# Four gated cross-attention layers on one core: attentions that begin by batch, and maxima spread four heads ahead

## The chip, the cores and the metric

The kernel runs on one core of a Trainium2 chip. The metric is the device time of one execution in microseconds (us). Engines are TensorE (PE, with its weight loads as PEld), VectorE (DVE), ScalarE (ACT), GpSimd (POOL) and SyncE (SP, which here issues DMAs). Each engine runs its own queue in order; they wait for each other by semaphores.

## The reference, cut to what matters

```python
x = x + tanh(g_xattn[0]) * xattn0(layernorm(x), ctx, mask)     # softmax over keys, mask of query x key
x = x + tanh(g_ffn[0])   * ffn0(layernorm(x))                  # 8 experts, each takes its top 256 tokens
x = x + tanh(g_xattn[1]) * xattn1(layernorm(x), ctx)           # softmax over the heads
x = x + tanh(g_ffn[1])   * ffn1(layernorm(x))                  # product of int8-quantised operands
x = x + tanh(g_xattn[2]) * xattn2(layernorm(x), ctx, padding)  # softmax over keys
x = x + tanh(g_ffn[2])   * ffn2(layernorm(x))                  # ternary weights, 256-1024-1024-1024-256
x = x + tanh(g_xattn[3]) * xattn3(layernorm(x), ctx)           # softmax over the queries
x = x + tanh(g_ffn[3])   * ffn3(layernorm(x))                  # 8 experts, two for each token
```

x and ctx are 8 x 256 x 256 (batch, rows, width) in fp32; every attention has 16 heads of width 16.

## The kernel before

All 2048 rows of x stay in SBUF as 16 tiles of 128 rows; a *pair* is the two tiles of one batch. The eight layers follow each other; each engine has a function for each (`attention`, `ffn0` to `ffn3`), run in the order of `STAGES`.

Layernorm: VectorE takes statistics of a tile (`statistics`, L1766, right behind each residual), then a chain of nine small operations for all 16 tiles at once with one square root on ScalarE (`layernorm`, L1782 to L1792), then normalises pair by pair (`normed`, L1816). TensorE transposes a pair (`turn_normed`, L751) and ScalarE copies it to `XNT` (L1434). Ahead of an attention, pairs 0 to 3 are done first and pairs 4 to 7 behind the first projections.

An attention projects keys, queries and values of a batch on TensorE (L804, L822, L842). ScalarE takes keys and queries out of PSUM (`split_k`, `split_q`), and ScalarE and VectorE split them into three bf16 parts (`middle_*`, `rest_*`, `low_*`; L1857, L1862, L1866, L1870). Six DMAs from POOL's queue (L337) and six from SP's (L474) then pack the parts of all heads into `Kpack` and `Qpack`, 128 KB each, so that one bf16 product of 96 rows gives exact scores. Rings of three batches.

Attentions 0 and 2 (`keys`): TensorE makes scores with the queries on the partitions (`smax`, L859), into two PSUM banks; VectorE takes row maxima (`row_max`, L1904). In attention 0 a second product with the identity adds the mask (L862). The maxima of a batch are turned (`max_turn`, L873), split into two bf16 rows (`max_part` on ScalarE, `max_rest` on VectorE, L1909) and written into `Qpack` by two DMAs (`max_rows`, L490), so that the second scores with the keys on the partitions (`scores`, L888, mask L891) come out less their maximum; ScalarE takes exponentials (`exps`, L1486), TensorE multiplies with the values (`values`, L897). `slot_keys(b)` on each engine writes out the order of a batch: the maxima of batch b + 1 (six of them ahead of the first score, then one behind each score), the scores of b, the end of b - 1, the projections of b + 3. `divide`, `output_turn`, `output_back`, `output` and `residual` (L1957) close a batch.

Attention 1 works in 16 units of 128 rows (`unit1`), attention 3 in eight slots (`slot3`, column maxima `col_max` L1914, four banks).

On SP, `attention` first waits for x of the layer before (`ready_x`), then issues the loads of context, weights and biases. `ffn1` issues the loads that copy 11 MB of feed-forward 2's weights from DRAM to DRAM (`staged`); `ffn2` loads them. `ffn0` gathers and scatters rows in DRAM and reads x back at its end (L418).

## Time and profile before

| | us |
|---|---|
| median of 3 runs | 2004.47 |
| lowest, highest | 1999.73, 2005.33 |
| profiled execution | 2003.19 |
| its span | 2001.3 |
| busy PE, DVE, ACT, POOL | 1635.1, 1091.8, 836.1, 295.8 |

The span runs from the first to the last instruction of the profiled execution. Times of the timeline count from its start. In it attention 0 runs to about 279, feed-forward 0 to 479, attention 1 to 774, feed-forward 1 to 826, attention 2 to 1081, feed-forward 2 to 1443, attention 3 to about 1640 and feed-forward 3 to the end. A matmul's duration in the rows holds its latency; where several follow each other, the distance of their starts is what one costs.

### The profile page before, as it was taken

The page shows a single profiled execution, that of the slowest core. Times are in us where ns is not written, and L with a number is a line of the kernel's source. Part 1 is how long each engine was busy: PE and PEld are TensorE (multiplying, and loading weights), DVE is VectorE, ACT ScalarE, POOL GpSimd, SP SyncE. Part 2 cuts the span into 40 slices and gives each one's busy share as a digit, 9 for nine tenths or more (in the row PEclk, how much of TensorE's full clock was granted, in tenths as well). Part 3 has the DMA queues.
Part 4 walks back from the last instruction along what each step waited for, and adds up shares of the span by engine and source line. Part 5 has one row for each costly group of instructions (what it writes and reads, how often), then busy time and mean ns, then how long its engine had stood idle before and what let it go on. Part 6 is the DMA issues. An engine that isn't in the chain of part 4 may idle for free.

```text
span 2001.3 us, 29422 instructions
## 1 busy us (share of the span) xinstructions
PE 1635.1 (82%) x10560; PEld 1228.3 (61%) x10561; DVE 1091.8 (55%) x2125; ACT 836.1 (42%) x1848; POOL 295.8 (15%) x351
## 2 busy tenths in 40 slices
PE   4999971794778874478887999999979873999997
PEld 3677750683555542335554677787745452999997
DVE  5555627404699998656663444535469966222221
ACT  3554440232776742335554622212289951222221
POOL 1100000432121100101110000000022201233332
PEclk8999985897798977679998999999989975999999
DMA  7545232125633315465523100000186625422221
GB/s 149 70 69 79 39 128 120 35 40 116 95 49 58 49 15 181 120 87 76 70 33 156 80 1 0 1 1 1 31 122 99 109 70 207 156 37 37 37 37 27
DMA packets 82841, 144.32 MB, mean 72 GB/s; under 512 B 13930, under 2 KB 68722, under 8 KB 79346
## 3 DMA queue, kind: packets, MB, share of 16 engines
q1 hardware_dynamic: 62754, 102.86, 22.1%
q0 software_dynamic: 19968, 39.87, 12.7%
q8 instruction: 76, 1.25, 0.3%
q14 instruction: 43, 0.35, 0.1%
HBM read 75.63 MB, written 27.79 MB: 52 GB/s over the span
## 4 chain that ended last, share of the span: by engine, by line
PE 60%; DVE 24%; ACT 5%; issue 5%; DMA 4%; SPq 1%; POOL 0%; DVEq 0%; POOLq 0%; ACTq 0%
PE ps L1259 12%; PE ps L1364 7%; PE ps L1375 7%; PE ps L897 4%; PE ps L1246 3%; PE ps L948 3%; DVE probs L2001 3%; DVE mx L1904 3%; PE ps L888 3%; PE ps L1179 2%; PE ps L1169 2%; PE ps L859 2%; ACT pT L1491 2%; PE ps L751 2%; PE ps L804 2%
## 5 line engine op out<-in xcount | busy, mean ns | idle before, releaser
L1904 DVE TENSOR_REDUCE mx<-ps 128x2 f32<-128x512 f32 x256 | 170.2, 688 | 149.2 <-PE ps L862 76.0
L337 POOL DMA_DIRECT2D Kpack<-KP x192 | 101.4, 536 | 984.8 <-DVE KP L1866 913.5
L1486 ACT ACTIVATE pT<-ps 128x512 f32<-128x512 f32 x256 | 146.0, 595 | 167.0 <-PE ps L891 91.4
L888 PE MATMUL ps<-Qpack,Kpack 99*128 99x256 bf16 (+1 forms) x768 | 163.8, 283 | 29.5 <-ACT pT L1491 11.4
L859 PE MATMUL ps<-Kpack,Qpack 97*128 97x256 bf16 x512 | 118.4, 292 | 49.1 <-DVE mx L1904 27.0
L1364 PEld LDWEIGHTS ps<-xgT,XNT 128*128 128x128 f32 x1280 | 150.3, 193 | 2.0
L1364 PE MATMUL ps<-xgT,XNT 128*128 128x128 f32 x1280 | 150.4, 276 | 0.0
L1375 PE MATMUL ps<-w,mid 128*128 x640 | 144.6, 379 | 0.0
L1693 ACT ACTIVATE mid<-ps 128x512 f32<-128x512 f32 x80 | 43.4, 595 | 206.9 <-PE ps L1364 206.9
L888 PEld LDWEIGHTS ps<-Qpack,Kpack 99*128 99x128 bf16 (+1 forms) x768 | 67.8, 100 | 99.3 <-ACT pT L1491 38.5
L1491 ACT ACTIVATE pT<-ps,nmax 128x256 f32<-128x256 f32 x256 | 120.2, 551 | 19.1 <-DVE nmax L1914 18.7
L1375 PEld LDWEIGHTS ps<-w,mid 128*128 128x128 f32 x640 | 118.6, 190 | 14.4
L1259 PE MATMUL ps<-partB,h 128*128 128x512 f32 x512 | 119.9, 395 | 1.3 <-ACT xn L1668 1.3
L1259 PE MATMUL ps<-partA,h 128*128 128x512 f32 x512 | 120.3, 396 | 0.0
L897 PE MATMUL ps<-pT,V 128*32 128x256 f32 x1536 | 112.0, 407 | 8.9 <-ACT pT L1486 6.5
L1259 PEld LDWEIGHTS ps<-partB,h 128*128 128x128 f32 x512 | 96.2, 188 | 24.3 <-ACT xn L1668 1.4
L1259 PEld LDWEIGHTS ps<-partA,h 128*128 128x128 f32 x512 | 96.3, 188 | 23.3 <-issue 0.5
L1668 ACT ACTIVATE xn<-ps,sc 128x512 f32<-128x512 f32 x64 | 43.2, 687 | 156.6 <-PE ps L1259 156.6
L1500 ACT ACTIVATE probs<-ps 128x512 f32<-128x512 f32 x128 | 77.3, 616 | 65.4 <-PE ps L980 65.0
L859 PEld LDWEIGHTS ps<-Kpack,Qpack 97*128 97x128 bf16 x512 | 45.9, 101 | 90.0 <-DVE mx L1904 61.7
L978 PE MATMUL ps<-Qpack,Kpack 96*128 96x256 bf16 x256 | 69.9, 296 | 30.9 <-DVE m L1976 28.7
L751 PE MATMUL ps<-ident,xn 128*128 128x128 f32 x224 | 41.9, 354 | 62.0 <-DVE xn L1816 52.7
(302 smaller groups left out, 3305.4 us busy)
## 6 DMA issues: line engine op xcount, KB each, us to landing
Kpack<-KP POOLq DMA_DIRECT2D x192, 128.0 KB, 5.2
Qpack<-QP SPq DMA_DIRECT2D x192, 128.0 KB, 7.1
w<-in_w SPq DMA_DIRECT2D x16, 1024.0 KB, 6.0
ctxT<-in_ctxT SPq DMA_DIRECT2D x32, 256.0 KB, 7.6
h<-h_rows SPq DMA_DIRECT2D x2, 4096.0 KB, 22.2
wd<-in_wd SPq DMA_DIRECT2D x4, 1536.0 KB, 14.4
xn_rows<-xn SPq DMA_DIRECT2D x16, 256.0 KB, 2.5
wu<-in_wu SPq DMA_DIRECT2D x4, 768.0 KB, 11.2
```

Source lines behind the costliest of these rows:

```text
L337: eng.dma_start(Kpack[j][DH * k:DH * (k + 1)].rearrange("d (e f) t -> d e (f t)", f=HALF), KP[par][:, part]).then_inc(done, 16)
L751: last = pe.transpose(bank[:, c, tt * P:(tt + 1) * P], src[:, tt, c * P:(c + 1) * P], eye[:])
L859: mm = pe.matmul(A[2 + h % 2][:, t], Qpack[j][0:MASK_ROW + 1, h, t * P:(t + 1) * P], Kpack[j][0:MASK_ROW + 1, h], start=True, stop=L != 0)
L888: mm = pe.matmul(A[h % ring][:, t], Kpack[par][0:rows, h, t * P:(t + 1) * P], Qpack[par][0:rows, h], start=True, stop=L != 0)
L897: mm = pe.matmul(O[c // 2][r0:r0 + VW, c % 2], V[par][:, t, h], weights[:, t], start=t == 0, stop=t == ST - 1)
L1259: mm = pe.matmul(bank, as_read(w[:, c, o * P:(o + 1) * P], x16), as_read(part[:, v, c], x16), start=v + c == 0, stop=v == 1 and c == HT - 1)
L1364: mm = pe.matmul(bank[:, f % 4 * P:(f % 4 + 1) * P], w1_tile[k % 2][:, c, f * P:(f + 1) * P], xgT3[k % 2][:, c], start=c == 0, stop=c == K ...
L1375: mm = pe.matmul(ps[5 + 2 * (k % 2)][:, 0], mid3[k % 2][:, c], w2_3[:, ds(e, 1), c].squeeze(1), start=c == 0, stop=c == HT - 1)
L1486: act.activation(pT[h % 8][:], A[h % 2][:], ACT.Exp).then_inc(s["exp_done"], 1)
L1491: e = act.activation(pT[h][:, t], A[h % 4][:, t], ACT.Exp, bias=nmax[:, t, h:h + 1], accum_out=esum[:, t, h:h + 1])
L1500: act.activation(probs[u % PROB_RING][:, 2 * k:2 * k + 2], A[(n_ - 1) % 4][:], ACT.Exp).then_inc(s["sc1_done"], 1)
L1904: dve.tensor_reduce(mx[:, :, h], A[2 + h % 2][:], AX.X, ALU.max).then_inc(s["smax_done"], 1)
```

## The change

- The layernorm of an attention begins with its first pairs (`HEAD`: one for attentions 0 and 1, two for 2 and 3). The chain is run twice, for the first tiles and for the rest (`deviations`), and pairs are normalised, transposed and copied one by one (`normed_pair`, `turn_pair`, `pair_out`); the rest of them stands behind the first scores: in attentions 0 and 2 inside `slot_keys`, in attention 1 inside `unit1` 0 and 1, in attention 3 inside `slot3(0)`.
- x is loaded in pieces of 2, 7 and 7 tiles, at the start and behind feed-forward 0.
- First keys (attention 1), or first keys and queries (attentions 2, 3), are projected and split inside the feed-forward ahead. For this the buffers of weights, context and splits (`pre`) no longer share memory with feed-forward 0 and 1, and SP issues the loads (`loads`) earlier: for attention 1 before it waits for feed-forward 0's scatters, for attention 2 at the start of feed-forward 1, for attention 3 in the last chunk of feed-forward 2.
- The DRAM to DRAM copies of feed-forward 2's weights go from the start of feed-forward 1 into attention 1's slots, three to five DMAs a batch.
- Attentions 0 and 2: the maxima run four heads ahead of the scores in one sequence over all batches (`MAX_AHEAD`), one maximum and one score in turn; the other steps of a slot get new places on all engines.
- Attention 0: the maxima's product with the mask (L862) goes; the mask is added on VectorE, in a `tensor_tensor_reduce` for each half of a head in place of one `tensor_reduce` for both.

```diff
@@ -42,6 +42,9 @@
 SOFTMAX_KEYS = (0, 2)
 PACK_RING, CTX_RING = 3, 4
 PROB_RING, UNITS1, AHEAD1 = 3, B * ST, 3
+HEAD = {0: 1, 1: 1, 2: 2, 3: 2}
+MAX_AHEAD = 4
+X_PIECES = (0, 2, 9, NT)
...
                         sp.wait_ge(s["v_psum"], 8 * i + b + 1)
                         load_ctx(b + CTX_RING, b % CTX_RING)
+                    for name in staged_in[b]:
+                        sp.dma_start(staged[name][:, b % HT], a[name][:, b % HT]).then_inc(s["f2_staged"], 16)

                 if L == 1:
                     packs1(0)
@@ -534,6 +567,8 @@
                         sp.wait_ge(s["xn_ready"], PAIRS * n + LNB * t + j + 1)
                         sp.dma_start(normed[:, ds(ST * (LNB * t + j), ST)], xn[j][:]).then_inc(xn_out[j], 16)

+            staged_in = [["h1_2", "h2_2", "w3_2"] + ["w1_2", "w2_2"] * (b < KC) for b in range(B)]
             def ffn(n, L):
...
@@ -737,6 +773,15 @@

             rt_order = {L: i for i, L in enumerate([L for k, L in stages if k == "ffn" and L in (0, 3)])}

+            def turn_pair(n, pair):
+                L = stages[n][1]
+                pe.wait_ge(s["xn_ready"], PAIRS * n + pair + 1)
+                pe.wait_ge(s["xnt_done"], PAIRS * n + LNB + max(pair - 1, 0))
+                for tt in range(ST):
+                    for c in range(KC):
+                        last = pe.transpose(turned_in(L, pair)[:, c, tt * P:(tt + 1) * P], normed_in(L, pair)[:, tt, c * P:(c + 1) * P], ident[:])
...
+                                       Kpack[j][0:MASK_ROW + 1, h], start=True, stop=True)
                     mm.then_inc(s["smax_ps"], 1)
+                def turn_later(b):
+                    pe.wait_ge(s["smax_done"], 16 * (8 * m_order[L] + b - 3) + H - 1)
+                    turn_pair(n, b)
...
-                pe.wait_ge(s["xnt_done"], PAIRS * n + LNB + 1)
-                proj_q(0)
-                for pair in range(LNB, PAIRS):
-                    turn_normed(n, LNB, pair - LNB)
-                pe.wait_ge(s["w_loaded"], w_total)
-                proj_v(0, 0)
-                proj_k(1, 1, 0)
-                pe.wait_ge(s["xnt_done"], PAIRS * (n + 1) + LNB)
-                proj_q(1)
                 if L == 0:
-                    pe.wait_ge(s["mask_ready"], 1)
+                    pe.wait_ge(s["qk_loaded"], qk_total(i))
+                    proj_k(0, 0, 0)
+                if HEAD[L] == 1:
+                    turn_pair(n, 0)
+                    proj_q(0)
+                    proj_k(1, 1, 0)
+                    turn_pair(n, 1)
+                    proj_q(1)
+                elif L == 3:
+                    pe.wait_ge(s["q_evac"], 8 * i + 2)
+                    pe.wait_ge(s["k_evac"], 8 * i + 2)
+                if not keys:
+                    pe.wait_ge(s["w_loaded"], w_total)
+                    proj_v(0, 0)
+                if L == 3:
+                    pe.wait_ge(s["f2_y"], NT)
                 if keys:
                     for h in range(H):
                         smax(0, h)
+                        if h == 3:
+                            pe.wait_ge(s["w_loaded"], w_total)
+                            proj_v(0, 0)
+                        if h == 7:
+                            turn_pair(n, 2)
+                        if h == 9:
+                            turn_pair(n, 3)
+                        if h == 11:
+                            proj_k(2, 2, 0)
                     max_turn(0)
-                    proj_k(2, 2, 0)
+                    for h in range(MAX_AHEAD):
+                        smax(1, h)
                     proj_q(2)
+                    if L == 0:
+                        pe.wait_ge(s["mask_ready"], 1)
...

                     def maximum(h):
-                        if nearer:
-                            smax(b + 1, h)
-                    maximum(0)
-                    maximum(1)
-                    if before:
-                        values(b - 1, 1 - par, CH - 1)
-                    for h in range(2, 6):
-                        maximum(h)
-                    if before:
-                        output_turn(b - 1)
-                    for h in range(10):
+                        if exists(b + 1 + h // H):
+                            smax(b + 1 + h // H, h % H)
+                    for h in range(H):
+                        maximum(h + MAX_AHEAD)
                         score(h)
-                        maximum(h + 6)
-                        if h == 3 and before:
-                            output_back(b - 1)
+                        if h == 1 and before:
+                            values(b - 1, 1 - par, CH - 1)
+                        if h == 4 and before:
+                            output_turn(b - 1)
                         if h == 5:
                             values(b, par, 0)
-                            if before:
-                                output(b - 1)
+                        if h == 6 and before:
+                            output_back(b - 1)
                         if h == 7 and nearer:
                             proj_v(b + 1, (b + 1) % CTX_RING)
-                    values(b, par, 1)
-                    score(10)
-                    if nearer:
-                        max_turn(b + 1)
-                    if later:
-                        proj_k(b + 3, (b + 3) % CTX_RING, (b + 3) // CTX_RING)
-                    score(11)
-                    score(12)
-                    if later:
-                        proj_q(b + 3)
-                    score(13)
-                    values(b, par, 2)
-                    score(14)
-                    score(15)
+                        if h == 8 and before:
+                            output(b - 1)
+                        if h == 9:
+                            values(b, par, 1)
+                        if h == 11 and exists(b + LNB):
+                            turn_later(b + LNB)
+                        if h == 11 and later:
+                            proj_k(b + 3, (b + 3) % CTX_RING, (b + 3) // CTX_RING)
+                        if h == 11 and nearer:
+                            max_turn(b + 1)
...
+                for p in range(2):
+                    turn_pair(n + 1, p)
+                pair(3, 1, False)
+                proj_q(0)
+                pair(4, 0, False)
+                proj_q(1)
+                for b in range(5, B):
+                    pair(b, b % 2, False)

...
+                if HEAD[L] == 1:
+                    deviations(chains[n], slice(0, ST))
+                    if L == 0:
+                        split_k(0, 0, 0)
+                    pair_out(n, 0)
+                    if L == 0:
+                        middle_k(0, 0)
+                    split_q(0, 0, 0)
+                    middle_q(0, 0)
+                    if L == 0:
+                        act.wait_ge(s["gates_loaded"], 32)
+                        act.activation(tg[:], gb[:], ACT.Tanh).then_inc(s["tg_ready"], 1)
+                    split_k(1, 1, 0)
+                    deviations(chains[n] + 1, slice(ST, NT))
+                    pair_out(n, 1)
...

                 def slot_keys(b):
                     before, nearer, later = exists(b - 1), exists(b + 1), exists(b + 2)
                     par = b % 2
-                    if later:
-                        split_k(b + 2, par, 0)
-                    if before:
-                        outputs_out(b - 1, 1)
-                    if later:
-                        split_q(b + 2, par, 0)
-                        middle_k(b + 2, par)
-                        middle_q(b + 2, par)
                     for h in range(H):
                         exps(b, h)
-                        if h == 4 and before:
+                        if h == 0 and later:
+                            split_q(b + 2, par, 0)
+                        if h == 1 and later:
+                            middle_k(b + 2, par)
+                        if h == 2 and before:
+                            outputs_out(b - 1, 1)
+                        if h == 3 and later:
...
                     m = 8 * m_order[L] + b
                     dve.wait_ge(s["smax_ps"], 16 * m + h + 1)
-                    dve.tensor_reduce(mx[:, :, h], A[2 + h % 2][:], AX.X, ALU.max).then_inc(s["smax_done"], 1)
+                    if L != 0:
+                        dve.tensor_reduce(mx[:, :, h], A[2 + h % 2][:], AX.X, ALU.max).then_inc(s["smax_done"], 1)
+                        return
+                    masked = Vb[0][:].bitcast(BF16).rearrange("p t (k s) -> p (t k) s", s=S)
+                    for t in range(ST):
+                        e = dve.tensor_tensor_reduce(masked[:, 2 * (h % 2) + t], A[2 + h % 2][:, t], mask_bf[:, 0, t], 1.0, NEG_EXP,
+                                                     ALU.add, ALU.max, mx[:, t, h:h + 1])
+                    e.then_inc(s["smax_done"], 1)

...
-                    low_q(b, b)
-                    if b == 0:
+                if HEAD[L] == 1:
+                    if L == 0:
                         constants()
-                        take_values(0, 0)
+                    dve.wait_ge(s["x_load0"], 16 * (1 + L))
+                    for t in range(ST):
+                        statistics(t)
+                    deviations(n, chains[n], slice(0, ST))
+                    normed_pair(n, 0)
+                    if L == 0:
+                        biases(0)
+                        rest_k(0, 0)
+                        low_k(0, 0)
+                    rest_q(0, 0)
+                    low_q(0, 0)
+                    dve.wait_ge(s["x_load1"], 32 * (1 + L))
+                    for t in range(ST, NT):
+                        statistics(t)
+                    if L == 1:
+                        dve.sem_inc(s["x_ffn"], 1)
+                    deviations(n, chains[n] + 1, slice(ST, NT))
+                    normed_pair(n, 1)
+                    rest_k(1, 1)
+                    normed_pair(n, 2)
+                    low_k(1, 1)
+                    normed_pair(n, 3)
+                    rest_q(1, 1)
+                if L != 0:
+                    constants()
+                if L == 0:
+                    masks()
+                    low_q(1, 1)
+                    dve.wait_ge(s["mask_ready"], 1)
+                elif L == 1:
+                    output_bias()
+                    low_q(1, 1)
...
+                            output_bias()
+                            take_values(0, 0)
                     max_rest(0)
+                    rest_k(2, 0)
+                    for h in range(MAX_AHEAD):
+                        row_max(1, h)

                 def slot_keys(b):
                     before, nearer, later = exists(b - 1), exists(b + 1), exists(b + 2)
                     par = b % 2
                     for h in range(H):
-                        if nearer:
-                            row_max(b + 1, h)
+                        ahead = h + MAX_AHEAD
+                        if exists(b + 1 + ahead // H):
+                            row_max(b + 1 + ahead // H, ahead % H)
+                        if h == 1 and later:
+                            rest_q(b + 2, par)
                         if h == 2 and later:
-                            rest_k(b + 2, par)
+                            low_k(b + 2, par)
                         if h == 4 and later:
-                            rest_q(b + 2, par)
-                        if h == 5 and later:
-                            low_k(b + 2, par)
-                        if h == 6 and before:
+                            low_q(b + 2, par)
+                        if h == 5 and before:
                             divide(b - 1)
-                        if h == 7 and later:
-                            low_q(b + 2, par)
-                        if h == 12 and before:
+                        if h == 7 and exists(b + LNB):
+                            normed_pair(n, b + LNB)
+                        if h == 8 and nearer:
+                            take_values(b + 1, 1 - par)
+                        if h == 10 and before:
                             residual(b - 1)
                         if h == 13 and nearer:
-                            take_values(b + 1, 1 - par)
-                    if nearer:
-                        max_rest(b + 1)
+                            max_rest(b + 1)
...
+                pair(0, 0)
+                pair(1, 1)
+                rest_k(0, 0)
+                deviations(n + 1, chains[n + 1], slice(0, 2 * ST))
+                normed_pair(n + 1, 0)
+                normed_pair(n + 1, 1)
+                low_k(0, 0)
+                pair(2, 0)
+                rest_k(1, 1)
+                pair(3, 1)
+                low_k(1, 1)
```

## Rows read from the trace of the kernel before

**Rows 1.** Busy time by stretch: stretch, length, PE, PEld, DVE, ACT, POOL (instructions), clock, DMA share, GB/s.
```profile
61.00:216.00 155.00, 147.74 (x1271) 112.69 (x1272) 87.43 (x160) 81.55 (x160) 18.83 (x36) 1.00 0.52 75
...
550.00:740.00 190.00, 156.43 (x1160) 99.83 (x1158) 186.19 (x207) 125.96 (x251) 23.34 (x36) 0.91 0.30 45
...
886.00:1023.00 137.00, 114.40 (x868) 73.64 (x867) 82.16 (x162) 73.25 (x149) 23.58 (x36) 0.94 0.51 69
...
1500.00:1600.00 100.00, 89.09 (x665) 51.44 (x665) 91.60 (x192) 93.78 (x375) 23.30 (x36) 0.97 0.65 105
```

**Rows 2.** Timeline, start: start, us, engine, line, operation, out<-in, count [idle before <-releaser].
```profile
6.92 2.71 DVE L1766 BATCH_NORM_STATS2 ln_st<-X 128x6 f32<-128x256 f32 x8 [6.77 <-DMA X<-in_x]
...
14.25 2.67 DVE L1816 TENSOR_SCALAR xn<-X,ln_tmp 128x256 f32<-128x256 f32 x8
...
16.21 0.60 ACT L1434 ACTIVATE XNT<-ps 128x512 f32<-128x512 f32 x1 [2.28 <-PE ps L751]
...
25.92 0.69 DVE L1870 TENSOR_TENSOR QP<-qr,QP 128x512 bf16<-128x512 f32 x1
...
41.87 0.69 DVE L1904 TENSOR_REDUCE mx<-ps 128x2 f32<-128x512 f32 x1 [6.70 <-PE ps L862]
```

**Rows 3.** Timeline, attention 0 in the steady state: two residuals, and products.
```profile
187.29 0.74 DVE L1957 SCALAR_TENSOR_TENSOR X<-ps,tg,X 128x512 f32<-128x512 f32 x1
...
210.40 0.27 PE L862 MATMUL ps<-mask_bf,ident_bf 128*128 128x256 bf16 x1
210.51 0.27 PE L859 MATMUL ps<-Kpack,Qpack 97*128 97x256 bf16 x1
...
216.27 0.74 DVE L1957 SCALAR_TENSOR_TENSOR X<-ps,tg,X 128x512 f32<-128x512 f32 x1
...
216.36 1.89 PE L842 MATMUL ps<-wv,ctxT 128*128 128x256 f32 x8
```

**Rows 4.** Timeline: two-operand operations on VectorE, and an accumulator read on ScalarE.
```profile
207.54 0.76 DVE L1947 TENSOR_TENSOR Oq<-ps,rden 128x256 f32<-128x256 f32 x2
...
1472.20 0.19 ACT L1491 ACTIVATION_READ_ACCUMULATOR pT<-ps,nmax 128x1 f32 x1
1472.30 0.47 ACT L1491 ACTIVATE pT<-ps,nmax 128x256 f32<-128x256 f32 x1
```

**Rows 5.** Timeline of two residuals of attention 2; waits of PE in 890 to 1023.
```profile
995.98 0.74 DVE L1957 SCALAR_TENSOR_TENSOR X<-ps,tg,X 128x512 f32<-128x512 f32 x1
...
1023.35 0.74 DVE L1957 SCALAR_TENSOR_TENSOR X<-ps,tg,X 128x512 f32<-128x512 f32 x1
...
PE ps L859 <- DVE mx L1904: 13.5, 20, 1.1
PE ps L873 <- DVE mx L1904: 5.1, 5, 1.7
```

**Rows 6.** One packing in attention 2: POOL's timeline; DMA rate in 904 to 925, 40 slices.
```profile
903.96 3.36 POOL L337 DMA_DIRECT2D Kpack<-KP x6 [14.55 <-DVE KP L1866]
...
GB/s 0 0 148 195 211 164 141 125 148 103 111 129 187 90 115 115 148 107 176 105 146 127 146 132 139 172 153 10 0 0 0 0 16 16 0 0 0 0 0 0
```

**Rows 7.** Timeline: x read back, and the first score of attention 1.
```profile
467.60 1.00 SPq L418 DMA_DIRECT2D X<-x_rows  x2
...
505.64 4.88 PE L966 MATMUL ps<-Qpack,Kpack 96*128 96x256 bf16 x22 [9.48 <-DMA Qpack<-QP]
```

**Rows 8.** Timeline: feed-forward 1's first and last step, and attention 2's first maximum.
```profile
805.55 0.88 DVE L2284 SCALAR_TENSOR_TENSOR y<-ps,lscale,rscale 128x256 f32<-128x256 f32 x2 [3.73 <-PE ps L1205]
...
825.55 0.75 DVE L1766 BATCH_NORM_STATS2 ln_st<-X  x2
...
855.75 11.06 DVE L1904 TENSOR_REDUCE mx<-ps 128x2 f32<-128x512 f32 x16 [8.32 <-PE ps L859]
```

**Rows 9.** Timeline: feed-forward 2's last products, and attention 3's first column maximum.
```profile
1434.12 7.75 PE L1282 MATMUL ps<-w,partA 128*128 128x256 f32 x64
...
1471.10 0.69 DVE L1914 TENSOR_REDUCE nmax<-ps 128x2 f32<-128x512 f32 x1 [6.30 <-PE ps L888]
```

545 lines of the change are left out of this document (355 added, 190 removed).

## The prediction

> **What bounds the kernel now.** I read the page first, then a table of busy times by stretch, then for each attention the start (timeline), one slot in the steady state (timeline, waits) and the DMA view of one packing. The kernel is one dependent sequence of eight layers, so a stage is worth what its own bound engine gives. The stretches [rows 1] show four kinds of attention: in attention 0 TensorE is busy 147.7 of 155 us; in attention 2 it is busy 114.4 of 137 at a clock of 0.94, no engine is full; in attention 1 VectorE is full (186.2 of 190); in attention 3 ScalarE and VectorE nearly are (93.8 and 91.6 of 100). Ahead of each attention lies a stretch of some 28 to 50 us in which nothing is full: the layernorm of all 16 tiles, first projections, splits, and the packing by DMA.
>
> **A. Start of attention 0.** Before, all 16 statistics (8 of them cost 2.71 us), all eight normalised pairs (a pair about 0.67) and both splits stand ahead of the first maximum, which begins at 41.87; the split of batch 0's queries had ended at 26.6 (25.92 + 0.69) [rows 2]. After, pair 0 goes alone: x in a piece of 256 KB lands at about 4, keys are projected and split before the queries; I put the query split of batch 0 at 18.6 (statistics 0.7, the chain to the deviation 1.5, pair 0.7, key product on the cold clock 2.6, transposes 1, copy 0.6, query product 2, four half-wide activations 1.6, three more steps of 0.65 each, and the key's steps queued between on ScalarE). Then VectorE must do 14 statistics (4.8), a second chain (1.5) and pair 1 (0.7) before batch 1 can be projected and split, which the order of VectorE puts ahead of the first maximum, with the mask conversions (0.8): 18.6 + 7 to pair 1, + 5.5 to its split queries, + 2.3: first maximum at about 33.4. That is 8.5 earlier. Packing is no longer last: keys of batch 0 travel during the layernorm, and the queries alone take half of what [rows 6] shows for both. The tanh and its table change lie under VectorE's statistics. Of the 8.5 I take 8; bounds 5 and 12.
>
> **B. Attention 0, mask in the maximum.** Removed on TensorE: the mask product of the maxima, 2 a head, 256 in all. Neighbouring matmuls start 0.11 apart [rows 3], so 32 x 0.11 = 3.6 us of a slot of 29.0 (two residuals apart [rows 3]). Added: two tensor_tensor_reduce of 128x256 a head in place of one tensor_reduce of 128x512, which costs 0.69 [rows 2]. The trace has no tensor_tensor_reduce. From below: two tensor_tensor of as many elements out of PSUM take 0.76 [rows 4]. From above I take twice that, 1.5, in case the reduction halves the rate. ScalarE reads its accumulator in a row of its own, 0.19 long, 0.10 to the next start [rows 4]; if VectorE does the same, a head costs 2 x (0.35 + 0.10) = 0.90, and I take that, as the structure is the nearest. VectorE's other work in a slot is four splits at 0.61, divide 1.15, residual with statistics 1.5, values 0.8, maximum row 0.4 and now a pair 0.67: 7.2. VectorE then has 16 x 0.90 + 7.2 = 21.6 a slot, TensorE 29.0 - 3.6 + 0.45 (a pair's transposes, moved here) = 25.9 with the 2 us of gaps it has now. The queues now alternate one maximum and one score, with ScalarE's query split, two middles and an output copy in the first four heads: exponentials 5 x 0.55 and this 3.9 against TensorE's 5.3, a stall of about 1. So 26.5 to 27 a slot: 2.2 x 5 full slots, 2.5 in slot 5 and 1 in slot 6, where VectorE (18.2) takes over from TensorE (16.1): 14. Bounds: -8 (1.46 a head, VectorE 30.6 a slot) and 24.
>
> The Trainium skill, "VectorE: DVE Perf Modes", section on the errata (fixed extra latency per instruction), speaks against this edit: every VectorE instruction out of PSUM pays 120 cycles plus one per element, so two halves cost more than one whole. By its figures two of 256 are an estimated 0.78 us against 0.66 for one of 512, 2 us more of VectorE in a slot. The rows agree on the direction (0.76 in [rows 4] to 0.69 in [rows 2]). The same page, on two instructions with no wait between them, counts an instruction that writes an accumulator as two; no row here shows that on VectorE.
>
> **C. Attention 2, maxima spread.** A slot lasts 27.4 and TensorE waits for maxima 13.5 + 5.1 us in 133 by the list of waits [rows 5], 3.8 a slot, and more through weight loads. Before, six maxima come in a bunch on two banks. Spread, TensorE's filler work lies between them. Its own work is about 20 at full clock. What is late next: ScalarE in the first four heads (6.6 against 4.2 on TensorE, 2.4), the row of maxima, which now leaves VectorE at head 13 and needs two DMA issues and 1.8 us to land, some 3.0, against 2.5 of product, maxima and score queued behind it (0.6). So I count 2.8 a slot for five slots and 2 in total behind: 16. Bounds 3 and 30.
>
> Maximum b+2 now begins at head 12 of slot b, so both packings must have landed by then. One packing takes 14 us from the key's first issue at 120 to 140 GB/s [rows 6]; key split at 3.5 in the slot, so 17.5, and TensorE reaches head 12 at 16 to 18. I cost it at 0; without that cover it is 1 to 4 a slot.
>
> **D. Attention 1.** The load is issued at 467.60 and the first product comes at 505.64 [rows 7]. After, the first 256 KB land about 2.8 us before the first megabyte did, weights and keys are ready, and the chain is: pair 0 split 10.5, 14 statistics and chain and pair 1 another 6.9, its transposes, copy, product, split 5.5, values 1.9: 24.8 behind 470.4, so 495.2, 10.4 earlier. Four pairs (2.7 us) move under a full VectorE [rows 1]: net 7.5; bounds 2 and 12. The copies of feed-forward 2's weights (11 MB) move from the transition into SP's queue behind each batch; SP's next packing waits some 20 us for its split there, so I cost them at 0.
>
> **E. From feed-forward 1 to attention 2.** First result 805.55, last statistics end at 826.3, first maximum 855.75 [rows 8]. After, keys, queries, splits and packing of batches 0 and 1 run inside feed-forward 1. The first result comes 1.9 later (a key product ahead), VectorE has 20.8 as before + 8 splits 5 + chain 1.5 + two pairs 1.35, + 1 of waits: it ends at about 837.4. The queries of batch 0 are split 9 us before that and land in time. With the two memsets (1.0) the first maximum is at 838.6: 17; bounds 12 and 20. Six pairs and a chain move behind the scores; the two among them that fall in the maxima of batch 0 are paid back by a product and a transposition less before the first score.
>
> **F. From feed-forward 2 to attention 3.** TensorE is full in feed-forward 2, so two pairs (1.0) and four projections (4 x 1.75, [rows 3] has 1.89 for eight) lengthen it by 8.1. The last layer's products began at 1434.12 [rows 9], so packing begins at 1442.2 and both packings take 13.5: first column maximum at 1456.4 against 1471.10, 14.7. Against it: ScalarE waits for the second chain ahead of its first exponential and loads its table then (3.0), and six copies of 0.60 fall in its full slot 0 (3.6): 8; bounds 3 and 15.
>
> **Sum.** 8 + 14 + 16 + 7.5 + 17 + 8 = 70.5. The profiled execution took 2003.19 (span 2001.3): 1932.7; the median of the runs is 1.3 above it, so 1934.
>
> **Rivals.** (1) VectorE bounds attention 0, at 1.3 to 1.5 us a head: B gives +3 to -8, so the gain is 48 to 60, time 1951, chance 0.13. For it: two instructions for one, no row. Against: two operations of that size at 0.76 [rows 4]. (2) Packing comes late for head 12 or the maxima row late for the first score: 2 to 3 a slot in both, C 4, B 5: 1955, chance 0.15. For it the 17.5 against 16 to 18. (3) Attentions 1 and 3 take back what their starts gave, as their engines are full: D 2, F 3: 1944, chance 0.10. (4) It does more than I count: all engines fill TensorE's gaps, B 24, C 30: 1910, chance 0.07. (5) Slower than before: a tensor_tensor_reduce of 128x256 that takes 0.9 us or more, 3 to 4 cycles an element. Attention 0 would be 128 heads x 1.8 + 7 x 7.2 + 17 for the last slot = 298 from the first maximum, against 237 now; that eats the 56.5 of the other parts. At 1.1 us it is 2060. Chance 0.07, of which 0.05 slower and 0.02 the same. (6) The forecast: 0.48.
>
> A measurement of this kernel can tell about 0.3% from no change. Faster 0.93, same 0.02, slower 0.05. The range takes in rivals 1 to 3 and 4 in part, and B and C at their low ends together: 1895 to 1970.
>
> **What would show it.** A: first maximum at 33, not 42. B: tensor_tensor_reduce near 0.4 with a short row behind it, slots of 26.5 to 27. C: slots of 24.6, waits of TensorE for maxima under 1 a slot. D, E, F: first score 25, first maximum 33 after feed-forward 1's first result, first column maximum 22 after the last layer's first product. Wrong if TensorE waits at head 12 for a DMA, if a slot of attention 0 has VectorE over 95% busy, or if attentions 1 and 3 are longer by more than 5 us from first score to end.

## The result and the profile after

The changed kernel took 1978.52 us (median of 4 runs, 1970.61 to 1979.44) where the kernel before took 2004.9 on the same chip: a ratio of 0.9864, interval 0.9832 to 0.9896. A second set gave 1982.12 (6 runs) against 2001.65: 0.9892, interval 0.9869 to 0.9916. So it is 20 to 26 us faster, not 70, and beyond the upper end of the range (1970).

The two profiled executions of the changed kernel (spans 1977.2 and 1980.8) against the one before, by the milestones that the forecast used; lengths in us:

```
stretch                                   forecast   before   after   after again
start to attention 0's first maximum        -8        41.9     35.0     36.6
attention 0, first maximum to last residual -14      236.5    235.3    238.0
last residual to feed-forward 0's logits     0        18.5     25.1     22.0
logits to attention 1's first score         -10.4    208.7    203.9    204.8
attention 1, first score to last residual   +2.7     267.5    271.2    268.2
to attention 2's first maximum              -17       82.7     65.8     65.7
attention 2, first maximum to last residual -16      224.1    219.8    219.6
to attention 3's first column maximum       -14.7    391.3    383.8    383.0
attention 3, first maximum to last residual +6.6     164.4    174.2    177.0
feed-forward 3                               0       365.8    363.1    366.0
```

One row is right to 0.1 us (E). Attention 0 gave 1.2 and -1.5 and attention 2 some 4.4, where 30 was counted for the two, attention 3 lost 10 to 13 us, and a stretch that the change doesn't touch, the routing of feed-forward 0, is 3.5 to 6.6 us longer. Apart from E's and most of A's, the gains are smaller than counted or given back elsewhere, so each had to be traced. Feed-forward 3, which no edit here touches, is between 360.0 and 366.1 long in the seventeen profiles of this document, so a difference of a few us in the total alone says little.

Busy times in the three attentions (columns as in [rows 1]). The kernel before:

```profile
41.87:278.40 236.53, 219.87 (x1860) 160.81 (x1858) 124.23 (x228) 114.89 (x222) 18.83 (x36) 0.99 0.42 62
855.75:1079.80 224.05, 183.01 (x1350) 112.26 (x1348) 127.51 (x248) 112.76 (x222) 29.26 (x44) 0.90 0.42 56
1471.10:1635.50 164.40, 143.79 (x1046) 83.29 (x1045) 137.97 (x293) 144.34 (x573) 29.02 (x44) 0.93 0.56 86
```

and the changed kernel:

```profile
34.97:270.30 235.33, 205.38 (x1636) 143.90 (x1636) 137.50 (x623) 115.16 (x228) 18.87 (x36) 0.94 0.39 60
836.30:1056.00 219.70, 180.15 (x1382) 116.79 (x1380) 133.97 (x274) 113.55 (x229) 29.34 (x44) 0.94 0.39 54
1439.87:1614.10 174.23, 145.61 (x1070) 86.12 (x1069) 143.91 (x315) 148.70 (x581) 29.08 (x44) 0.94 0.47 75
```

In attention 0 TensorE's busy time fell by 14.5 us, although 256 products at 0.11 (28 us) are gone: the granted clock fell from 0.99 to 0.94, and six pairs' transpositions (2.7) and a values product (1.9) now stand in this stretch. Its idle time rose from 16.7 to 30.0, which leaves 1.2 of the 14.5.

The slots themselves came out nearly as forecast. VectorE's timeline, residuals as in [rows 3] and [rows 5], and the new maximum:

```profile
35.32 0.42 DVE L2104 CUSTOM_DVE_ANT_0 Vb<-ps,mask_bf 128x256 bf16<-128x256 f32 x1
35.66 0.08 DVE L2104 DVE_READ_ACCUMULATOR2_ANT mx<- 128x1 f32 x1
35.66 0.42 DVE L2104 CUSTOM_DVE_ANT_0 Vb<-ps,mask_bf 128x256 bf16<-128x256 f32 x1
...
185.50 0.75 DVE L2159 SCALAR_TENSOR_TENSOR X<-ps,tg,X 128x512 f32<-128x512 f32 x1
...
212.02 0.75 DVE L2159 SCALAR_TENSOR_TENSOR X<-ps,tg,X 128x512 f32<-128x512 f32 x1
...
978.78 0.74 DVE L2159 SCALAR_TENSOR_TENSOR X<-ps,tg,X 128x512 f32<-128x512 f32 x1
...
1003.54 0.74 DVE L2159 SCALAR_TENSOR_TENSOR X<-ps,tg,X 128x512 f32<-128x512 f32 x1
```

Four full slots of attention 0 are 26.5, 28.3, 27.3 and 26.5 long where all were 29.0, those of attention 2 25.4, 24.8, 26.1 and 24.8 where they were 27.4. A tensor_tensor_reduce starts 0.35 after the one before it, the read of its accumulator (0.08) lies under the next one. What the slots gained, the stretch from the first maximum to the first residual gave back: 58.5 to 68.4 in attention 0 and 57.9 to 66.1 in attention 2. (The residual also stands three heads later in its slot, which moves a few us from the last distances into the first; the sums over an attention are free of that.)

### The profile page after: what moved, and what is told of

Read it like the earlier page. It is cut to its first block, busy times and chain, and to the rows that moved or that the text cites. A ratio compares the mean times of both kernels' runs of the same rounds, so it can differ in the third digit from the quotient of the medians.

```text
span 1977.2 us, 29280 instructions
## 1 busy us (share of the span) xinstructions
PE 1612.8 (82%) x10304; PEld 1214.1 (61%) x10305; DVE 1106.3 (56%) x2541; ACT 834.3 (42%) x1854; POOL 296.8 (15%) x351
## 4 chain that ended last, share of the span: by engine, by line
PE 56%; DVE 24%; ACT 7%; issue 6%; DMA 5%; SPq 1%; POOL 0%; DVEq 0%; POOLq 0%; ACTq 0%
PE ps L1361 12%; PE ps L1469 7%; PE ps L1480 7%; PE ps L1330 4%; DVE probs L2203 3%; DMA Qpack<-QP 3%; PE ps L1004 2%; PE ps L1241 2%; PE ps L861 2%; ACT pT L1605 2%; PE ps L1251 2%; PE ps L951 2%; PE ps L942 2%; PE ps L890 2%; PE ps L1386 2%
## 5 line engine op out<-in xcount | busy, mean ns | idle before, releaser
L1600 ACT ACTIVATE pT<-ps 128x512 f32<-128x512 f32 x256 | 151.9, 607 | 185.0 <-PE ps L945 98.0
L942 PE MATMUL ps<-Qpack,Kpack 99*128 99x256 bf16 (+1 forms) x768 | 166.4, 283 | 19.7 <-ACT pT L1605 9.9
L911 PE MATMUL ps<-Kpack,Qpack 97*128 97x256 bf16 x512 | 102.9, 287 | 40.4 <-DVE mx L2104 11.4
L1480 PEld LDWEIGHTS ps<-w,mid 128*128 128x128 f32 x640 | 118.6, 190 | 14.5
L2104 DVE CUSTOM_DVE_ANT_0 Vb<-ps,mask_bf 128x256 bf16<-128x256 f32 x256 | 94.8, 419 | 52.2 <-PE ps L911 52.1
L2100 DVE TENSOR_REDUCE mx<-ps 128x2 f32<-128x512 f32 x128 | 84.3, 686 | 46.2 <-PE ps L911 45.6
L2116 DVE TENSOR_REDUCE nmax<-ps 128x2 f32<-128x512 f32 x128 | 83.4, 683 | 26.2 <-PE ps L942 26.0
```

Source lines behind the costliest of these rows:

```text
L911: mm = pe.matmul(A[2 + h % 2][:, t], Qpack[j][0:MASK_ROW + 1, h, t * P:(t + 1) * P], Kpack[j][0:MASK_ROW + 1, h], start=True, stop=True)
L942: mm = pe.matmul(A[h % ring][:, t], Kpack[par][0:rows, h, t * P:(t + 1) * P], Qpack[par][0:rows, h], start=True, stop=L != 0)
L1480: mm = pe.matmul(ps[5 + 2 * (k % 2)][:, 0], mid3[k % 2][:, c], w2_3[:, ds(e, 1), c].squeeze(1), start=c == 0, stop=c == HT - 1)
L1600: act.activation(pT[h % 8][:], A[h % 2][:], ACT.Exp).then_inc(s["exp_done"], 1)
L2100: dve.tensor_reduce(mx[:, :, h], A[2 + h % 2][:], AX.X, ALU.max).then_inc(s["smax_done"], 1)
L2104: e = dve.tensor_tensor_reduce(masked[:, 2 * (h % 2) + t], A[2 + h % 2][:, t], mask_bf[:, 0, t], 1.0, NEG_EXP, ALU.add, ALU.max, mx[:, t, ...
```

## The experiments

All but e2 start from the changed kernel. For clock effects I use one figure, worked out from the tables of busy time by stretch: TensorE's busy time times (1 - granted clock), summed over pieces of half a microsecond. It is an estimate of how much of the busy time is there only because the clock was at 1.2 GHz (neighbouring products of 128x256 start 0.11 apart in [rows 3] and 0.21 apart in e5 from 82 to 84, where the granted clock is 0.50), and is called the low-clock part below.

In the total, e1 (0.9935) lies above the two sets of the changed kernel (ratios 0.9864 and 0.9892), e8 (0.9919) above the first and within the interval of the second, and e13, e14 and e15 lie below both. All other edits to it have 0.9871 to 0.9903, which can't be told from no change. What is said of those rests on stretches of one profile each.

### e1 and e2: the mask in the maximum (B), alone

```diff
-                                       Kpack[j][0:MASK_ROW + 1, h], start=True, stop=True)
+                                       Kpack[j][0:MASK_ROW + 1, h], start=True, stop=L != 0)
+                        if L == 0:
+                            mm = pe.matmul(A[2 + h % 2][:, t], ident_bf[:], mask_bf[:, 0, t], start=False, stop=True)
```

e1 has the products back (with tensor_reduce for every L). 

> The changed kernel with part B alone undone: in attention 0 the maxima get their mask products back (256 of them) and the tensor_reduce. Theory 1 (my forecast's step: the mask in the maximum is worth 14 us and lies on the path): 1978.5 + 14 = 1992, with full slots of 28.5 to 29 in attention 0. Theory 2 (the products removed were what kept TensorE dense, and the granted clock fell for it: in the changed kernel TensorE's records at the lower clock hold 9.6 us more extra time in attention 0 and 6.0 us more in feed-forward 0 than before): the 28 us of products come back, but some 12 to 15 of slow clock go, so attention 0 is within 4 us of the changed kernel's 235.3, feed-forward 0's way to the logits falls from 25.1 to about 18.5, and the total is 1972 to 1982.

e2 is the kernel before with this edit alone. 

> The kernel before with part B alone done: mask added inside the maximum in attention 0, nothing else. Forecast's theory: with maxima still in bunches, TensorE loses 3.6 us of work a slot, VectorE is not the bound (0.69 a head), so 2 to 3 a slot: 2004.5 - 20 = 1985. Clock theory: TensorE gets gaps, the granted clock of attention 0 falls from 0.99 to about 0.94 and feed-forward 0 loses up to 6.5: 1992 to 2000. In both the tensor_tensor_reduce costs 0.35 from start to start.

e1: 1986.54 (ratio 0.9935, 0.9914 to 0.9957). e2: 1997.41 (0.9980, 0.9965 to 0.9995). Attention 0 of e1 and of e2:

```profile
35.40:276.70 241.30, 220.73 (x1891) 165.94 (x1889) 129.62 (x239) 115.62 (x228) 18.83 (x36) 0.99 0.39 58
```

```profile
41.90:272.70 230.80, 201.61 (x1606) 137.39 (x1604) 132.14 (x611) 114.19 (x222) 18.84 (x36) 0.94 0.43 63
```

The edit is worth 5.7 us in attention 0 on the old order (236.5 to 230.8) and 5.2 on the new one (241.3 to 236.1, 236.1 being the mean of the nine profiles with this code of attention 0, from 234.3 to 238.2). Of 28 us of products, in e2 12.5 became idle time (16.7 to 29.2) and 9.4 low-clock part (2.1 to 11.5). In e1 the low-clock part is 1.6, in the nine profiles 8.7 to 15.0, and the three longest of these attentions have the three largest. So the clock theory was right about the clock, in both directions (0.99 with the products, 0.94 without), but too strong on the time: attention 0 does not stay as it was. By the ratios e1 is 9 to 14 us slower than the changed kernel. Only the 5.2 lie in attention 0; in its one profile the rest lies in stretches that the edit doesn't touch (attention 3 is 179.4 long, against 174.2 and 177.0), so the 9 to 14 is not the price of the edit.

### e3: the maxima of batch 2 behind slot 0

```diff
-                        maximum(h + MAX_AHEAD)
+                        if b or h + MAX_AHEAD < H:
+                            maximum(h + MAX_AHEAD)
...
+                    if b == 0:
+                        for h in range(MAX_AHEAD):
+                            maximum(H + h)
```

VectorE's maxima move in the same way.

> The changed kernel, only the four maxima of batch 2 that stand among the last scores of slot 0 (attentions 0 and 2) moved behind slot 0. If the DMA wait of 3.65 us at head 12 of attention 0's slot 0 (and its like in attention 2) is a loss of its own, the last four scores go out before it and about 3 us are gained there, 1 in attention 2: 1974.5. If it only moves (the same four maxima must still run before slot 1's), 0 to 1: 1978.

1973.95 (ratio 0.9897, 0.9862 to 0.9932), which by the ratio is no gain. The wait at head 12 of the changed kernel, by its list of waits in 58 to 100,

```profile
PE ps L911 <- DMA Qpack<-QP: 3.6, 1, 3.6
```

is gone, and the first exponential to the first residual of attention 0 takes 41.7 where the changed kernel has 44.0 and 45.3 (and no other profile with this slot 0 less than 43.6). Attention 2 shows nothing (221.0 to 219.7). So this wait costs 2 to 4 us, once, by one profile.

### e4 and e10: fillers on TensorE around feed-forward 0's routing

e4 puts 16 of 128x256 ahead of the first pair, e10 six of 128x128 behind each pair's router products:

```diff
+                if L == 0:
+                    for k in range(WARM0):
+                        pe.matmul(O[0][:, k % 2], ident_bf[:], mask_bf[:, 1, k % 2], start=True, stop=True)
...
+                if stages[n] == ("ffn", 0):
+                    for k in range(FILL0):
+                        pe.matmul(O[0][:, k % 2, 0:P], ident_bf[:], ident_bf[:], start=True, stop=True)
```

> The changed kernel with 16 matmuls of 128x256 that nobody reads put on TensorE's queue between attention 0's last output product and feed-forward 0's first transposition, where TensorE idles 4.9 us. Clock theory: feed-forward 0's transpositions and router products (25.1 us from the last residual to the logits, at a granted clock of 0.50 from 276 to 294; 18.6 in the kernel before, at up to 1.00) run at the full clock in part and save 3 to 6 us: 1973 to 1975. Rival (the fillers only delay, or the clock stays): 1978 to 1980.

> The changed kernel with 6 matmuls of 128x128 (bf16, nobody reads them) behind each pair's router products in feed-forward 0, where TensorE is busy without a gap for 20 us and yet runs at a granted clock of 0.50, the router products being only 8 columns wide. Theory a (what is granted follows the kind of work, and narrow products do not raise it): with wider work mixed in, the clock rises behind the first pairs and the stretch from the last residual to the logits takes 18 to 19.5 us in spite of 3 us more of work; total 1974 to 1978. Theory b (chance of the phase alone: 18.5, 22 or 25 in any kernel): the stretch is one of those, plus 3 to 5 us for the fillers: total 1981 to 1985.

The changed kernel in that stretch, and e10 (columns as in [rows 1]):

```profile
276.00:278.00 2.00, 2.00 (x12) 2.00 (x10) 1.26 (x5) 1.20 (x2) 0.00 (x0) 0.50 0.88 295
...
282.00:284.00 2.00, 2.00 (x11) 2.00 (x10) 0.00 (x0) 0.60 (x1) 0.00 (x0) 0.50 1.08 307
...
288.00:290.00 2.00, 2.00 (x11) 2.00 (x11) 0.00 (x0) 0.57 (x1) 0.00 (x0) 0.50 1.01 430
```

```profile
281.00:283.00 2.00, 2.00 (x13) 2.00 (x11) 1.26 (x4) 1.28 (x3) 0.00 (x0) 0.53 0.99 331
283.00:285.00 2.00, 2.00 (x24) 2.00 (x24) 1.91 (x7) 0.91 (x2) 0.00 (x0) 1.00 0.78 282
...
293.00:295.00 2.00, 1.36 (x17) 1.18 (x14) 0.71 (x3) 0.00 (x0) 0.00 (x0) 1.00 0.95 399
```

TensorE is busy without a gap in the changed kernel from 276 to 294 and stays at 1.2 GHz. The stretch took 18.5, 18.9, 21.7, 22.0 (nine times) or 25.1 us (three times) in the fifteen profiles without router fillers, with a low-clock part of 3.5, 6.7 or 10.0. With them it took 19.1 in e10 and 19.2 in e14 below, although TensorE has 48 products more to do, with a low-clock part of 1.4 and 1.5, less than any other. e4 had 22.0 like most: its fillers end before the pairs begin. So the fillers keep the clock up, on two profiles, as theory a had it. But the kind of work doesn't decide it alone: in the kernel before, the same instructions without fillers ran at 1.00 from 288 to 292. What decides between 18.5, 22.0 and 25.1 stays open. In the total neither edit shows: 1976.54 (0.9877) and 1977.83 (0.9895).

### e6 and e7: attention 3's packing, one batch after the other, or held

```diff
+                    if L == 2 and b == 1:
+                        sp.wait_ge(s["smax_ps"], 16 * 8 * m_order[L] + 1)
+                    if L == 3 and b == 1:
+                        sp.wait_ge(s["st_ps"], 16 * 8 * s_order[L] + 1)
                     queries_out(b, j)
```

This is e7 on SP's queue; GpSimd waits likewise ahead of pack_batch(1). e6 waits for batch 0's packing semaphores instead. e5, the changed kernel once more, ran beside them.

> The changed kernel as it is, for its median and for which of its losses come back in a second profile. Clock theory: the stretch from the last residual of attention 0 to the logits takes 18.5, 22.0 or 25.1 us from run to run of whatever kernel, in steps of about 3.3; total 1970 to 1980. The losses that belong to the program come back to 0.5 us: TensorE idle for 11 to 12 us before attention 3's values product and 5 us behind its first scores, and 3.6 us at head 12 of attention 0's slot 0.

> The changed kernel, with batch 1's packing begun in attentions 2 and 3 only when batch 0's has landed, so that the two no longer share the DMA engines. Theory 1 (attention 3's first score waits for packing): batch 0's twelve transfers land in about 8 us instead of 18 and the first column maximum comes 6 to 8 us earlier: 1971. Theory 2 (TensorE is held by its own instruction stream: it idles 11.6 us before the values product with no semaphore left to wait for, and goes on 1.8 us after one packet of 16 KB of the instruction queue, which travels while all 16 DMA engines are at 0.99): the engines are as full as before until both batches are packed, so nothing changes in attention 3: 0 to 2 us, 1976 to 1978. Attention 2 in both: first maximum bound by VectorE's last statistics at 834.7, so 1.5 earlier.

> The changed kernel, with batch 1's packing held until the first scores (attention 3) or the first maximum product (attention 2) of batch 0 have been issued. Theory 2 (instruction packets queued behind packing): the DMA engines run empty some 8 us after attention 3's packing begins, the packet comes at once, TensorE's idle time before the values product falls from 11.6 to 3 us or less and the 5.0 us behind the first scores may stay or move; first column maximum 8 us earlier, total 1969. Theory 1 (batch 0's packing alone): the same 8 us, so it is told from theory 2 by the run with serial packing beside it. Rival 3 (batch 1 now comes late for slot 1, or the later packs meet batch 2's): slot 0 of attention 3 is longer by as much: 1977.

Medians: e5 1982.12, e6 1972.73 (0.9871, 0.9847 to 0.9895), e7 1973.83 (0.9873, 0.9845 to 0.9901); the ratios are not clear of the changed kernel's. The chain of waits of the changed kernel there (start, length, what):

```profile
1417.94 6.12 PE ps L1386 x51
1424.07 11.58 issue
1435.65 3.75 PE ps L890 x8
1439.40 0.43 PE ps L942 x2
1439.83 0.43 PE ps L843
1440.26 4.99 issue
1445.25 0.59 PE ps L843
```

TensorE stands for 11.6 us ahead of the values product, whose semaphores had long been reached, and for 5.0 in the middle of one key product, between its two passes. e5 repeats both (10.6 and 4.7).

In the first of these stretches lies one instruction, a branch. Feed-forward 2's end stands in the program twice, in an `If` and its `Else` (L1401; L1297 in the kernel before, L1409 in e7), and TensorE leaves the one that ran by a jump over the other. The view of that line (duration of the four branches in ns, smallest, median and largest) in the kernel before, in the changed kernel and in e7:

```profile
L1297 PEldq COMPARE_BRANCH  x4: 79/1714/3416, 1118.1 to 1439.6; - x4
```

```profile
L1401 PEldq COMPARE_BRANCH  x4: 79/1954/13610, 1094.4 to 1421.8; - x4
```

```profile
L1409 PEldq COMPARE_BRANCH  x4: 79/1874/10530, 1088.7 to 1416.0; - x4
```

The largest is the last one in all three. It takes 3.4 us in the kernel before, where the DMA engines are at 0.02 and packing begins 17 us later, and 13.6 in the changed kernel, where packing began 5 us before it. In the half microsecond from 1432.0 the DMA view of the changed kernel has one packet of an instruction queue among the packing:

```profile
q8 instruction: 1, 0.02, 19.8%
```

It travels at 1432.2 and TensorE goes on at 1435.65; the next one is at 1442.8, before 1445.25. In all fifteen profiles of the changed order TensorE goes on 1.7 to 2.2 us after the first packet has ended, and in the ten with the second stall 1.2 to 1.7 us after the second one. In e7 the DMA engines run empty at 1424.0, and in the half microsecond up to there is TensorE's packet:

```profile
q8 instruction: 1, 0.02, 14.1%
```

```profile
1422.00:1424.00 2.00, 0.00 (x0) 0.00 (x0) 0.00 (x0) 0.00 (x0) 0.00 (x0) 0.50 1.13 168
1424.00:1426.00 2.00, 0.00 (x0) 0.00 (x0) 0.00 (x0) 0.00 (x0) 0.00 (x0) 0.50 0.02 6
```

```profile
1426.79 3.75 PE L898 MATMUL ps<-wv,ctxT 128*128 128x256 f32 x8 [8.50 <-issue]
1430.34 0.63 PE L950 MATMUL ps<-Qpack,Kpack 96*128 96x256 bf16 x2
1430.76 1.06 PE L851 MATMUL ps<-ctxT,wk 128*128 128x256 f32 x2
```

The second stall is gone there, the next packet (1427.2) finding idle engines; e6, which starts batch 1's packing as soon as batch 0's has landed, keeps it (4.1). So theory 2 holds in its second half: TensorE's instructions queue behind the packing. Its first half was too hopeful: the idle time fell only to 8.5 and the branch to 10.5, because batch 0's twelve transfers alone take until 1424.0. No run held batch 0's packing until the branch was past. Attention 3's first stretch (first column maximum to first residual) is 47.4 in e7 where e5 has 51.8 and e6 51.1, and its first maximum is 2.2 earlier. e4 and e10 confirm it: they differ from the changed kernel only by TensorE instructions in feed-forward 0, which shift where its packets end (this is also why I take the queue for TensorE's), and their stretches are 47.3 and 47.1, with no stall in the key product; all ten others in which batch 1's packing is not held (51.1 to 54.0) have it, 4.1 to 6.0 long. Attention 2 nets nothing in e6 and e7 (first maximum 1.6 earlier, then 1.4 more to the first exponential).

### e8: the weight copies back in feed-forward 1

```diff
-                    for name in staged_in[b]:
-                        sp.dma_start(staged[name][:, b % HT], a[name][:, b % HT]).then_inc(s["f2_staged"], 16)
...
                     sp.dma_start(rhs1[:], a["rhs1"]).then_inc(s["f1_rhs"], 16)
+                    for name in ternary:
+                        sp.dma_start(staged[name], a[name]).then_inc(s["f2_staged"], 16)
...
```

> The changed kernel with one thing undone: the copies of feed-forward 2's weights (11 MB) are issued in feed-forward 1 again and not behind each batch of attention 1. If they cost attention 1 what it gave back (first score to end 271.2 us against 267.5 before), attention 1 is 3 to 4 us shorter. In feed-forward 1 they now stand ahead of the packing of attention 2's first batches, so its first maximum comes 5 to 20 us later: total 1980 to 1995. If the copies are free in attention 1, its 271 stays, and only the second part is seen.

1985.48 (0.9919, 0.9899 to 0.9940). Attention 1 is 268.3, against 268.2 in e5, and attention 2's first maximum comes 10.4 later after attention 1's end (76.1 to 65.7). The copies are free where the change put them; my cost of 0 for them stands, and attention 1's give-back has another cause.

### e9 and e13: the way of the maximum row

```diff
-                        if h == 14 and later:
+                        if h == 15 and later:
                             proj_q(b + 3)
...
+                        if h == 12 and nearer:
+                            max_part(b + 1)
                         if h == 12 and exists(b + 3):
                             split_k(b + 3, 1 - par, 0)
-                        if h == 13 and nearer:
-                            max_part(b + 1)
```

The first edit alone is e9. The second, on ScalarE's queue, with VectorE's max_rest moved to h == 12 likewise, is e13.

> The changed kernel; in attentions 0 and 2 the query product of batch b+3 stands one head later, behind the last score of the slot and not behind score 14. In the changed kernel TensorE waits there for VectorE's rest of the maximum row, which frees the bank: 3.3 us in attention 0 and 5.1 in attention 2, waits that the kernel before did not have. If they are part of what ate the gain of the spread maxima, TensorE's idle time in attention 2's slots falls from 25 to 21 and the slots of 24.8 to 26.2 become 24 to 25: total 3 to 5 us less than the changed kernel. Rival: TensorE then waits as long for something else at that place (exponentials, the maximum row for the next slot's first score), and the slots stay within 0.2 us.

> The changed kernel; in attentions 0 and 2 ScalarE's and VectorE's two halves of the maximum row stand behind head 12 of the slot, ahead of the key split, not behind head 13, so that the row and the bank that it frees come one head and four activations earlier, some 2 to 3 us. If the way of the maximum row is what gives the spread's gain back (TensorE waits 5.1 us for that bank in attention 2 and 3.3 in attention 0, and when the query product was moved behind it, 5.0 and 3.3 for the row's DMA instead), both waits go: slots of 24.8 in attention 2 become 23.8, those of 27.3 in attention 0 become 26.5, and the kernel gains 6 to 10 us: 1970 to 1974 where the changed kernel has 1980. Rival: TensorE is then full or waits for exponentials in the same places: under 2 us.

TensorE's waits in attention 2 (what waited for what, us, times, longest) in the changed kernel, 905 to 1056:

```profile
PE ps L861 <- DVE MR L2111: 5.1, 4, 1.3
PE ps L927 <- DVE mx L2100: 4.3, 2, 2.2
...
PE ps L911 <- DVE mx L2100: 2.1, 4, 0.5
...
PE ps L942 <- DMA Qpack<-MR: 1.3, 1, 1.3
```

in e9, same stretch:

```profile
PE ps L942 <- DMA Qpack<-MR: 5.0, 6, 2.5
...
PE ps L861 <- DVE MR L2111: 0.8, 3, 0.3
```

and in e13, 897 to 1043, where the first of these lines is missing:

```profile
PE ps L942 <- DMA Qpack<-MR: 1.7, 2, 1.0
```

The spread took the 18.6 us of waits for maxima of [rows 5] down to 6.4, and a new one came: the query product waits for the bank that VectorE's rest of the maximum row frees. Moving the product (e9, 1979.64, 0.9903) turned it into a wait for the row's DMA, and attention 2's slots stayed (25.4, 24.8, 26.1, 25.6); attention 0's fell by 0.2. Moving the row itself one head and four activations forward (e13) cut slots to 23.8, 23.3, 24.6, 24.0 and 25.4, 25.4, 26.1, 25.4, and the total to 1966.71: 0.9818, 0.9792 to 0.9845. Attention 0 went from 236.1 (mean of nine) to 229.7, attention 2 from 219.6 to 216.0 (219.5 to 228.0 in the eight profiles with the changed kernel's attention 2). This one edit is worth 9 to 15 us by the ratios. It was rival (2)'s second half, which I had put at 0.6 a slot and 0.15 of chance.

### e11: x ahead of the keys' packing in attention 1

```diff
+                if L == 1:
+                    pool.wait_ge(s["x_load0"], 32)
                 pack_batch(0)
```

> The changed kernel; GpSimd packs the keys of attention 1's batch 0 only when the first piece of x has landed (now it issues them 1.3 us before x is loaded, and the first statistics begin 4.1 to 5.5 us after the load's issue, where my forecast had 2.8 for a quarter of the size). If the packing delays x, the first statistics begin 2.8 us after the issue and attention 1's first score 1.3 to 2.7 us earlier. Rival: no change, since the fixed part of a load is most of it, or the keys are packed too late, as the first maxima's product needs them 30 us later (they have room), 0.

1974.93 (0.9880, 0.9857 to 0.9904). In the changed kernel the load is issued at 465.82 and the statistics begin at 471.30; in e11:

```profile
462.54 1.50 SPq L442 DMA_DIRECT2D X<-x_rows  x3
...
465.68 3.29 POOL L345 DMA_DIRECT2D Kpack<-KP  x6 [5.23 <-DMA X<-x_rows]
...
465.41 0.75 DVE L1949 BATCH_NORM_STATS2 ln_st<-X 128x6 f32<-128x256 f32 x2 [4.21 <-DMA X<-x_rows]
```

2.9 us after the issue and not 4.1 to 5.5: the packing had delayed x. The first score comes 3.0 earlier (30.9 behind the load's issue, 33.9 in e5), and attention 1 is 271.1 long and not 268.2. That looks as if all of it were taken back, but the profile of the changed kernel and e4's have 271.2 too, without an earlier start, and slots of the same lengths: 1.0 more than e5 to the first residual and 2.0 more in the last four distances. Nor is the 3.0 firm: e14 below has this edit and its first score is 32.9 behind the issue, e13 doesn't have it and has 32.1. Together, from the routing's logits to attention 1's last residual, e11 takes 472.6, the changed kernel 475.1 and 473.0, the kernel before 476.2 and (e2) 473.7. So the edit gains nothing that can be told from no change.

### e12: attention 3's second chain first

```diff
-                        if b == 0 and h == 1:
-                            deviations(n, chains[n] + 1, slice(2 * ST, NT))
...
+                    deviations(n, chains[n] + 1, slice(2 * ST, NT))
                     slots_keys(slot3)
```

> The changed kernel; in attention 3 VectorE does the second chain of the layernorm's deviations ahead of the first column maximum, in its idle time of 10 to 13 us there, not behind the second maximum. In the changed kernel ScalarE waits for that chain and then loads its table ahead of its first exponential, which comes 9.2 to 9.5 us after the first column maximum against 0.7 in the kernel before. My forecast priced this at 3.0. If it is what makes slot 0 longer (first column maximum to first residual 51.9 against 39.2), the first exponential comes 1 us behind the first maximum and 5 to 8 us are gained: 1971 to 1974. If TensorE's own stall of 4.7 us behind the first scores (instruction packets) covers it, 1 to 3 us.

1978.7 (0.9897, 0.9878 to 0.9916). The first exponential, 9.5 us behind the first column maximum in the changed kernel (1449.38 to 1439.87), is 0.7 behind it (maximum at 1432.90):

```profile
1433.63 0.47 ACT L1605 ACTIVATE pT<-ps,nmax 128x256 f32<-128x256 f32 x1 [9.61 <-DVE nmax L2116]
```

and the first residual is not a microsecond earlier (52.1, e5 51.8): TensorE's stall in the key product is 6.0 here, and by that the one hides the other.

### e14 and e15: mended together

e15 is held packing, early row and chain first; e14 has x first and the router fillers as well.

> The changed kernel with the held second packing, attention 3's second chain ahead of its first maximum, x before the keys' packing in attention 1, the early maximum row and the router fillers together. By the single runs: held packing -7, early row -6 to -10 if it works, fillers 0 to -3, chain 0 alone but up to -5 where TensorE no longer stalls behind the first scores, x first 0: 1962 to 1968 where the changed kernel has 1980. If the attentions' engines take the starts back as in the run with x first, 1972.

> As the run before, without the router fillers and without x first. If the fillers are worth their 3 us in the long run (they keep the granted clock up in feed-forward 0) this one is 3 us slower than the run with them; if not, they are the same to 1 us. Also the second look at the chain put first in attention 3: with held packing its first exponential comes 1 us behind the first maximum and slot 0 is 3 to 5 us shorter than the 47.4 that held packing alone gave.

e14: 1955.0 (0.9758, 0.9731 to 0.9786). e15: 1953.76 (0.9752, 0.9732 to 0.9772), 49 us under the kernel before and about twice the gain of the change as it was. The three attentions in e15:

```profile
34.90:264.70 229.80, 204.20 (x1636) 144.37 (x1636) 137.63 (x623) 114.86 (x228) 18.85 (x36) 0.94 0.40 61
827.60:1042.10 214.50, 183.05 (x1380) 119.45 (x1380) 134.11 (x276) 113.61 (x229) 32.26 (x50) 0.92 0.44 59
1423.60:1589.60 166.00, 142.89 (x1070) 84.42 (x1068) 142.72 (x306) 146.99 (x579) 32.24 (x50) 0.96 0.56 87
```

Attention 3's first stretch is 44.0, 3.4 less than with held packing alone: with the stall gone the chain does cost, about the 3.0 that I had forecast. Fillers and x first together are worth nothing in the total, though e14's routing was 5.9 shorter than e15's in the profiles.

## Why the prediction was wrong, step by step

The two largest terms, B and C, failed by the same step: an attention was summed from its shorter slots, with its first stretch taken as unchanged and the late row of maxima at 0.6 a slot. They gave -1.5 to 1.2 and 4.4 where 30 was counted. F failed by the packing's length and by what else has to pass beside it, D by its load and its chain.

**A (8).** Right in kind: first maximum at 34.97 and 36.6, forecast 33.4, so 6.9 and 5.3. What it left out is that a values product (1.9) and six pairs (2.7 by the forecast's own 0.45 a pair) only moved behind the first maximum.

**B (14).** The slot of 26.5 to 27 came true (26.5 to 28.3), and 0.90 a head was too much: it is 0.69. The step that failed is the sum over an attention from its slots: 2.2 x 5 + 3 took the first stretch as unchanged. It is 9.9 to 11.9 longer, of which the later place of the residual is an estimated 5 (three heads of a slot of 26.5). There the moved work (1.9 + 2.7), the wait of 3.65 at head 12 (which I had costed at 0, for a cover of 17.5 against 16 to 18) and a part of the lower clock lie. Attention 0 as a whole gave 1.2 and -1.5. e2 shows the reason most plainly: removing work from the engine that bounds a stage opened gaps in it (12.5 of 28), and the granted clock fell with it (9.4 more). That it was the gaps which took the clock down is my reading; what e1 and e2 show is that it goes with the products.

**The routing behind it (0).** Not in my sum at all: 3.5 to 6.6 us. By the row-by-row clock it is the low-clock part (3.5 before, 6.7 and 10.0 after), and kernels with other edits show all three values. The kernel before was caught at the lowest; e2, which has the same code there, has 21.7. Executions of the changed kernel differ by 9 us in one set (1970.61 to 1979.44) and by 12 in the other (1973.29 to 1985.07), and the fastest had the highest mean clock (0.909 against 0.901 to 0.904 in the first set).

**C (16).** 4.3 and 4.5. "The row of maxima, which now leaves VectorE at head 13 ... (0.6)" is the term that was mis-sized: with the query product standing behind the same bank it held TensorE 5.1 + 1.3 us, and e13 got 3.6 of attention 2 and 6.4 of attention 0 back by it. As in B, the sum from the slots failed too: four full slots gave 8.6 together, 2.1 each where 2.8 was forecast, and the first stretch took 8.2 back. A part of that is the residual's later place, which the last slots return; another is moved work: at full clock TensorE has 5 us more to do in the stretch (180.15 less a low-clock part of 11.1, against 183.01 less 18.9). Of the 12 us that are missing, e13's 3.6 and this 5 make 9; the other 3 stay open. What remains of waits for maxima, 6.4, was forecast as under 1 a slot, rightly.

**D (7.5).** Two terms failed. The quarter load was not 2.8 faster: its statistics began 5.5 and 4.1 behind the issue where the whole megabyte had 5.6, because keys were being packed (e11 has 2.9). And the chain behind it, forecast at 24.8, took 28.0 and 29.9; TensorE's granted clock there was 0.63 and 0.62. Of the 3.9 to 4.8 that were left of 10.4, attention 1 took 0.7 to 3.7 back by the table. e8 rules the copies out. Attention 1's steady slots are 31.6 in every profile, before and after; what it gives back lies ahead of the first residual (95.5 before, 99.4 and 98.4 after), where the moved pairs are, forecast at 2.7. The length before is itself uncertain: e2, with the same attention 1, has 263.3 and not 267.4. By the sums over both stretches in e11's section D was worth -1.4 to 3.2, and the runs don't fix it closer.

**E (17).** 16.9 and 17.0. VectorE's last statistics of feed-forward 1 end at 833.6, two memsets at 834.7, first maximum at 836.30. That the sum is right to 0.1 is partly luck: the first result comes 3.3 later where 1.9 was forecast, VectorE takes 27.3 from there to its last statistics and not 30, and the first maximum is 2.7 behind them and not 1.2.

**F (8).** -2.3 and -4.3. "Both packings take 13.5" failed: that was the distance from batch 0's first issue to its first use (1456.87 to 1470.46). In the changed kernel batch 0's rows land 17.4 behind the first issue (1416.41 to 1433.83) and batch 1's 27.0; alone, in e7, batch 0's take 13.6. And the step took it that nothing but the packed rows is waited for. TensorE's branch out of feed-forward 2, done in 3.4 before packing began in the kernel before, now stands behind the packing and takes 13.6, the values product (3.75) comes behind it, and the stall of 5.0 in the first scores follows; none of this was in the sum. The 3.0 for ScalarE's chain was right in size, but only counts once that stall is gone (e12, e15).

**The rivals.** No single one came true. (2) did in both halves: the wait at head 12, once, and the late row in every slot. (3) did for attention 3 in size, but not by its reason: four slots are 19.7 to 20.0 long, 19.7 before, and the loss lies in the first stretch (39.2 to 51.9). Two mechanisms were not among the rivals, the clock and the instruction packets. Of the three signs that I had named for being wrong, two were there: TensorE waits at head 12 for a DMA, and attention 3 is more than 5 us longer. Rival (1) and rival (5) are out: VectorE is busy 137.5 of 235 us in attention 0, and a tensor_tensor_reduce takes 0.35. The range was too narrow at its upper end because it took the low ends of B and C and nothing for stretches that no edit touches.

## What to carry over

When an edit shortens the steady state, sum the whole stage: work moved behind a milestone, the first slot's new waits and the last slot have to be in it. When a queue's order is spread out, follow the longest chain that crosses engines (here the maximum row: TensorE, ScalarE, VectorE, two DMAs) and move its links up with it; a wait that one moves without its cause comes back at the next instruction. And hold a large transfer back if a tight one, or the instruction stream itself, has to pass at that time, above all where an engine is about to take a branch.

## What the runs showed of the hardware

- TensorE's instruction packets (16 KB; 75 in all, a median of 20 us apart) wait behind data transfers. With all 16 engines at 1.0 TensorE stood 9 to 12 us and then 4 to 6 with no semaphore to wait for, the second in ten of twelve profiles; the other two, with instructions shifted, had only the first. The first is a branch that jumps over unused code: 3.4 us in the kernel before and in e2, with idle DMA engines, and 10.5 to 14.1 in the fifteen profiles in which packing was under way. The Trainium skill, "Runtime: NRT & Kernel Launch", section on instruction fetch mechanics, says that a sequencer fetches its stream in 16 KiB blocks by a DMA queue of its own, that crossing a block is mostly hidden, and that a taken branch to a block not held stalls. The size agrees with the rows, and so does the stall at the branch. That crossing a block is hidden does not hold for the second stall, 4.1 to 6.0 in the middle of a product with full engines; it does in e7, where they are idle.
- TensorE can be busy without a gap for 18 us and stay at 1.2 GHz (0.50 from 276 to 294 in the changed kernel, over transpositions and router products); with six fillers a pair among them it was at 1.00 from 283 to 295 (e10). The kernel before had 1.00 from 288 to 292 without fillers.
- Removing 28 us of products from a stage that ran at 0.99 brought it to 0.94, and putting them back brought 0.99 again (e1, e2).
- A tensor_tensor_reduce of 128x256 out of PSUM starts 0.35 behind the last one, its accumulator read of 0.08 beside it. Two a head cost 0.69; the tensor_reduce of 128x512 costs 0.60 from start to start (two in 1.29). The Trainium skill, "VectorE: DVE Perf Modes", section on the errata, gave an estimated 0.12 more for two halves; the rows agree, with 0.09. What its section on two instructions with no wait between them says, that one which writes an accumulator counts as two, agrees in that there are two rows; the second one adds nothing to the distance of starts.
